# First layer's attention probabilities turned by DMA transposes instead of on the tensor engine

## The reference

```python
# layer 0, per image, C = 128, N = 1024
h = group_norm(x, gn_w, gn_b)                        # 32 groups of 4 channels
q, k, v = split(qkv_w @ h + qkv_b)                   # 128 channels each
attn = softmax(q.T @ k * C ** -0.5, axis=-1)         # 1024 x 1024
x = x + proj_w @ (v @ attn.T) + proj_b
# layer 1, per image, q and k have 16 channels
q, k, v = Wq @ x + bq, Wk @ x + bk, Wv @ x + bv
attn = softmax(q.T @ k, axis=-1)
x = gamma * (v @ attn.T) + x
```

## Time and profile before

| | |
|---|---|
| median of 3 runs | 1952.1 us |
| profiled execution, span | 1946.7 us |
| median less that span | 5.4 us |
| TensorE matmul busy | 1860.1 us (96%) |
| VectorE busy | 1592.0 us (82%) |
| ScalarE busy | 1479.8 us (76%) |
| GpSimd busy | 1071.3 us (55%) |
| DMA engines, mean | 18 GB/s |

### The profile page before, as it was taken

How to read it: one execution, slowest core, us unless ns; L and a number is a source line. 1 busy time by engine, 2 the same in 40 slices (tenths; PEclk the granted TensorE clock), 3 DMA queues, 4 the chain that set the end, 5 groups by cost and what they waited for, 6 DMA issues and landing times.

```text
span 1946.7 us, 36450 instructions
## 1 busy us (share of the span) xinstructions
PE 1860.1 (96%) x11145; PEld 1124.8 (58%) x11145; DVE 1592.0 (82%) x2707; ACT 1479.8 (76%) x2593; POOL 1071.3 (55%) x1000
## 2 busy tenths in 40 slices
PE   5899999999999999999999999999999999999997
PEld 3455565555565555565555555565655555655554
DVE  5688888888888888888888888888888888888875
ACT  4677778777777778777778777777787778777775
POOL 4455565555655556555555655556555555555533
PEclk9999999999999999999999999999999999999999
DMA  1000000000000000000000000000000000000000
GB/s 35 16 1 22 23 18 22 6 21 22 16 22 22 5 22 22 16 22 22 5 22 22 16 22 15 11 22 16 22 22 5 22 22 16 22 23 7 12 12 23
DMA packets 15898, 34.44 MB, mean 18 GB/s; under 512 B 2896, under 2 KB 3568, under 8 KB 15856
## 3 DMA queue, kind: packets, MB, share of 16 engines
q1 hardware_dynamic: 14704, 33.91, 4.9%
q10 hardware_dynamic: 1152, 0.00, 0.0%
HBM read 17.13 MB, written 16.78 MB: 17 GB/s over the span
## 4 chain that ended last, share of the span: by engine, by line
PE 55%; ACT 14%; issue 14%; DVE 12%; POOL 2%; ACTq 1%; DVEq 1%; DMA 0%; POOLq 0%
PE turned L801 14%; PE side L756 9%; PE side L757 8%; PE side L758 8%; ACT prob L408 7%; DVE nmax L542 4%; PE scores L787 4%; ACT pt_head L419 4%; ACT qk L444 3%; PE side L888 3%; PE scores L756 3%; PE scores L758 3%; PE scores L757 3%; DVE pt_tail L561 2%; DVE qk L622 2%
## 5 line engine op out<-in xcount | busy, mean ns | idle before, releaser
L294 POOL TENSOR_SCALAR prob<-prob,rinv 128x1024 f32<-128x1024 f32 x512 | 572.8, 1119 | 814.1 <-DVE rinv L550 803.1
L419 ACT ACTIVATE pt_head<-turned 128x512 f16<-128x512 f32 x1024 | 611.7, 598 | 238.4 <-PE turned L801 228.9
L561 DVE TENSOR_TENSOR pt_tail<-turned,pt_head 128x512 f16<-128x512 f32 x1024 | 700.3, 684 | 106.6 <-ACT pt_head L419 103.5
L801 PE MATMUL turned<-ident,prob 128*128 128x128 f32 x4096 | 625.9, 275 | 33.7 <-DVE pt_tail L561 17.4
L801 PEld LDWEIGHTS turned<-ident,prob 128*128 128x128 f32 x4096 | 489.4, 141 | 282.0 <-DVE pt_tail L561 123.1
L542 DVE TENSOR_REDUCE nmax<-scores 128x1 f32<-128x1024 f32 x512 | 622.1, 1215 | 20.7 <-PE scores L787 10.4
L408 ACT ACTIVATE prob<-scores,nmax 128x1024 f32<-128x1024 f32 x512 | 571.1, 1115 | 8.1 <-DVE nmax L542 6.3
L756 PE MATMUL side<-pt_head,v_head 128*128 128x512 f16 x1024 | 388.9, 380 | 26.2 <-DVE qk L622 17.6
L757 PE MATMUL side<-pt_tail,v_head 128*128 128x512 f16 x1024 | 388.5, 379 | 0.0
L758 PE MATMUL side<-pt_head,v_tail 128*128 128x512 f16 x1024 | 388.5, 379 | 0.0
L756 PE MATMUL scores<-qk_head 128*128 128x512 f16 x512 | 195.9, 383 | 7.1 <-ACT prob L408 4.8
(11 more groups left out here) (87 smaller groups left out, 1714.4 us busy)
## 6 DMA issues: line engine op xcount, KB each, us to landing
x_raw<-in_x_dram SPq DMA_DIRECT2D x32, 512.0 KB, 3.4
out_dram<-y SPq DMA_DIRECT2D x64, 256.0 KB, 2.3
w_qkv<-in_L_conv_qkv_w_dram SPq DMA_DIRECT2D x3, 64.0 KB, 3.7
w_proj<-in_L_conv_proj_w_dram SPq DMA_DIRECT2D x1, 64.0 KB, 3.6
w_v<-in_L_conv_Wv_dram SPq DMA_DIRECT2D x1, 64.0 KB, 3.5
b_qk<-in_L_conv_bq_dram SPq DMA_DIRECT2D x2, 0.1 KB, 3.0
gnw<-in_L_conv_gn_w_dram ACTq DMA_DIRECT2D x1, 0.5 KB, 4.1
gnb<-in_L_conv_gn_b_dram ACTq DMA_DIRECT2D x1, 0.5 KB, 4.4
```

What stands on the lines that cost most here:

```text
L294: nc.gpsimd.tensor_scalar(prob[layer][:, t % 2, :], prob[layer][:, t % 2, :], rinv[layer][:, t:t + 1], P_UP, ALU.mult, ALU.mult).then_inc( ...
L419: nc.scalar.activation(pt_head[layer][:, t // PER_HALF, PER_HALF * h:PER_HALF * (h + 1), at:at + C], turned[layer][:, :].rearrange("p (j n ...
L561: nc.vector.tensor_tensor(pt_tail[layer][part], turned[layer][:, :].rearrange("p (j n) -> p j n", n=C), pt_head[layer][part], ALU.subtract ...
L801: done = nc.tensor.transpose(turned[layer][:, j * C:(j + 1) * C], prob[layer][:, t % 2, m:m + C], ident[:, :])
```

## The change

It concerns layer 0 (lane 0) alone, with its 260 tiles. GpSimd writes the scaled probabilities as fp16 into a new tile `head_row` instead of in place. VectorE makes the fp16 tail in rows, `tail_row` = `prob` x (`rinv` x 4096) - `head_row`, in one instruction over 128 x 1024, from three operands in SBUF; a small instruction (`scale_up`) forms `rinv` x 4096 first. SP issues a DMA transpose of `head_row` and one of `tail_row` (256 KB each), which write all eight turned blocks into `pt_head` and `pt_tail`. The transposes of lane 0 on TensorE and the head and tail copies out of `turned` for lane 0 are gone. The tail in rows stands at the end of the same slot as the tile's maximum. Lane 1 is as before.

```diff
+CROSSBAR = (0,)
+            def swing(layer, it, k):                       # SP
+                im, t = tile_of(layer, it, k)
+                if no_tile(layer, im, t):
+                    return
+                h, at = t // PER_HALF, (t % PER_HALF) * C
+                sp.wait_ge(row_tailed[layer], im.n * TILES + t + 1)
+                sp.sem_inc(waited_sp, 1)
+                if t % PER_HALF == 0 and not (isinstance(im.n, int) and im.n == 0):
+                    sp.wait_ge(attended[layer], im.n * 2 + h - 1)
+                    sp.sem_inc(waited_sp, 1)
+                for rows, into in ((head_row, pt_head), (tail_row, pt_tail)):
+                    sp.dma_start_transpose(into[layer][:, h, :, at:at + C],
+                                           rows[layer][:, t % 2, :]).then_inc(swung[layer][t % 2][h], 16)
...
+                for k in range(8):                         # SP, body
+                    if k == 1 and not skip(second):
...
+                    if k == 4 and not skip(ahead):
+                        load_x(ahead)
+                    for layer in CROSSBAR:
+                        swing(layer, it, k)
+                    if k == 4 and not skip(first):
...
                 pool.wait_ge(inverted[layer], im.n * TILES + t + 1)       # normalise
                 stand_apart()
+                if layer in CROSSBAR:
+                    before = slot_user(im, t)
+                    if before:
+                        pool.wait_ge(swung[layer][t % 2][before[1] // PER_HALF], swings(*before))
+                        stand_apart()
+                    nc.gpsimd.tensor_scalar(head_row[layer][:, t % 2, :], prob[layer][:, t % 2, :],
+                                            rinv[layer][:, t:t + 1], P_UP, ALU.mult,
+                                            ALU.mult).then_inc(row_headed[layer], 1)
+                    return
...
+            def scale_up(layer, it, k):                    # VectorE
...
+                nc.vector.tensor_scalar(rinv_up[layer][:, t:t + 1], rinv[layer][:, t:t + 1], P_UP, 1.0,
+                                        ALU.mult, ALU.mult).then_inc(scaled_up[layer], 1)
+            def tail_row_out(layer, it, k):
...
+                dve.wait_ge(scaled_up[layer], im.n * TILES + t + 1)
+                dve.wait_ge(row_headed[layer], im.n * TILES + t + 1)
+                nc.vector.scalar_tensor_tensor(out=tail_row[layer][:, t % 2, :], in0=prob[layer][:, t % 2, :],
+                                               scalar=rinv_up[layer][:, t:t + 1],
+                                               in1=head_row[layer][:, t % 2, :], op0=ALU.mult,
+                                               op1=ALU.subtract).then_inc(row_tailed[layer], 1)
...
                     invert(1, it, k)
+                    for layer in CROSSBAR:
+                        scale_up(layer, it, k)
                     extra(it, k, 1)
...
                     pt_tail_out(1, it, k, 1)
+                    for layer in CROSSBAR:
+                        tail_row_out(layer, it, k)
...
                 if t == 0:                                                # attend
+                    if layer in CROSSBAR:
+                        for slot in range(2):
+                            pe.wait_ge(swung[layer][slot][h], im.n * 64 + 64)
+                    else:
+                        pe.wait_ge(pt_tailed[layer], im.n * 16 + 8 * (h + 1))
```

More of the change, by code:

```diff
@@ L134, in build @@
         rinv = [sb(f"rinv{l}", [C, TILES]) for l in range(2)]
+        head_row = [sb(f"head_row{l}", [C, 2, N], F16) for l in CROSSBAR]
+        tail_row = [sb(f"tail_row{l}", [C, 2, N], F16) for l in CROSSBAR]
+        rinv_up = [sb(f"rinv_up{l}", [C, TILES]) for l in CROSSBAR]
         pt_head = [sb(f"pt_head{l}", [C, 2, TILES, HALF], F16) for l in range(2)]
@@ L147, in build @@
         waited_dve = sem("waited_dve")
+        waited_sp = sem("waited_sp")
         zeroed = sem("zeroed")
@@ L185, in build @@
         pt_tailed = [sem(f"pt_tailed{l}") for l in range(2)]
+        row_headed = [sem(f"row_headed{l}") for l in CROSSBAR]
+        row_tailed = [sem(f"row_tailed{l}") for l in CROSSBAR]
+        scaled_up = [sem(f"scaled_up{l}") for l in CROSSBAR]
+        swung = [[[sem(f"swung{l}_{s}_{h}") for h in range(2)] for s in range(2)] for l in CROSSBAR]
         attended = [sem(f"attended{l}") for l in range(2)]
@@ L218, in no_tile, with swings, slot_user @@
             return not 0 <= t < PER_HALF if layer == 0 and last(im) else skip(im)
+        def swings(im, t):
+            return im.n * 64 + 32 * (t % PER_HALF // 2 + 1)
+        def slot_user(im, t):
+            if isinstance(im.n, int) and im.n == 0 and t < 2:
+                return None
+            return (im, t - 2) if t >= 2 else (im.before(2 // 2), t + 6)
         @block.sync
@@ L414, in pt_head_out @@
                 im, t = previous_tile(layer, it, k)
-                if no_tile(layer, im, t):
+                if no_tile(layer, im, t) or layer in CROSSBAR:
                     return
@@ L809, in attend @@
                 if t == 0:
-                    pe.wait_ge(pt_tailed[layer], im.n * 16 + 8 * (h + 1))
+                    if layer in CROSSBAR:
+                        for slot in range(2):
+                            pe.wait_ge(swung[layer][slot][h], im.n * 64 + 64)
+                    else:
+                        pe.wait_ge(pt_tailed[layer], im.n * 16 + 8 * (h + 1))
                     if layer == 0:
@@ L972, in _ @@
                 attend(1, end.before(2), 0, t)
-            pe.wait_ge(pt_tailed[0], IMAGES * 16 + 8)
+            for slot in range(2):
+                pe.wait_ge(swung[0][slot][0], IMAGES * 64 + 64)
             pe.wait_ge(qk1_tailed, IMAGES * 2)
```

25 lines of the change are left out of this document (15 added, 10 removed).

## The result

The changed kernel takes 2117.3 us (median of 4 runs, 2116.5 to 2119.0) against 1952.1 us: ratio 1.085, 95% interval 1.083 to 1.086. It is 165 us slower, where 1875 us was predicted, and outside the predicted range.

The account below looks back on a forecast made before the run. TensorE (56.2 of 59.0 us an iteration) was taken as the bound, passing to VectorE's order. 31 iterations x -2.9 = -90 and edges +13 gave a span of 1870, with 5.4 around it 1875 us; range 1785 to 2090.

Parts of the forecast that it names:

- TensorE as the bound: One middle iteration of the kernel before: TensorE's work sums to 56.2 of 59.0 us, 2.8 us lost to waits.
- VectorE's slot and the port: VectorE's slot after the change: 5.81 us by order, 6.52 with `tail_row` waiting for GpSimd's SBUF port.
- the base slot: A slot of the changed kernel without extra work, such as slot 6: 6.52 us, bounds 5.81 and 7.7.
- The rival of GpSimd's other instructions: GpSimd's instructions besides the scalings take the port too: 63 us an iteration, 2090 us, or 59.6 and 1984; chance 0.12.
- The port's sum: Port waits over the eight slots of an iteration: 55.4 us with the port, 53.0 without.
- The iteration: A full iteration of eight slots: 55.4 us plus 0.7 makes 56.1, 2.9 us less than 59.0.
- for coupling between engines I add 0.7: Allowance per iteration for engines waiting on each other: 0.7 us, where it was 2.8 before.
- The edges: First 12 slots, lane 0 alone: `head_row` and `tail_row` stand between exponential and next maximum, +13 us.
- The transposes: SP's DMA transposes, a pair per tile: landing after 3.2 us, hidden under a slot and before `attend`, cost 0.
- The choice of small packets' price: DMA transposes' 256-byte rows: 14 + 12 ns each rather than 104 ns, so 3.2 us a pair instead of 13.3.
- The rival with a chance of 0.17: SP's queue, each tile: transposes bound the slot; 13.3 us a pair gives 3460 us, 9 us gives 2340; chance 0.17.
- hold a pair for little: SP's queue, slots 0 and 4: loads and stores waiting for GpSimd delay a transpose pair only little.

Follow-up runs that it names:

- less_pe: The kernel before with one of four fp32 transposes per half of lane 0's tiles left on TensorE (first tile whole): 1895.7 us (0.971).
- no_tail: The changed kernel, unpadded, without `tail_row` and `scale_up`, both DMA transposes turning `head_row`: 1741.5 us (0.892).
- pad_after: The changed kernel with 32 semaphore increments ahead of VectorE's list, nothing else changed: 2059.3 us (1.054).
- no_port: pad_after with `tail_row` in two halves of 512 whose second operand is a zeroed PSUM bank instead of `head_row`: 2015.6 us (1.031).
- gn_first: pad_after with `tail_row` behind the group norm steps of slots 2, 5 and 7 instead of ahead of them: 2005.9 us (1.027).
- two_gn: pad_after with gn_first's order and lane 1's transposes alternating two PSUM banks, one of them lane 0's unused bank: 1969.4 us (1.009).
- third_turn: pad_after with a third DMA transpose for each tile, of `tail_row` into a spare tensor nobody reads: 2065.3 us (1.057).
- tail_lag: pad_after with `tail_row` and its two DMA transposes one slot later, behind maximum 0 of the next tile: 2301.1 us (1.177).
- pad_before: The kernel before with 40 semaphore increments ahead of VectorE's list, nothing else changed: 1981.2 us (1.015).
- act_head: two_gn with `head_row` made by ScalarE in place of GpSimd, and `scale_up` right behind reciprocal 0: 2031.1 us (1.040).
- tail_mid: pad_after with `tail_row` right behind `scale_up`, ahead of the extra work and lane 1's second half tail: 2069.4 us (1.061).

## Why the prediction was wrong

*TensorE as the bound (the first step, wrong).* The sum of its work, 56.2 of 59.0 us, was right and the conclusion from it was not. An iteration was read as one stage. By slots, TensorE had 6.1 to 7.8 us of work where the slots took 6.1 to 8.7. Slots 0, 3 and 5 had 0.7 to 1.8 us of slack; less_pe shows 1.9 of 5.2 us given back. This count of slack does not say which slot gives back: slot 0 gave 0.62 us and slot 3 nothing. The busy share of 96% could not tell: the matmul rows overlap (0.38 us each at a step of 0.22), so little idle time appears between them. With all three engines relieved and no tail, 6.75 us an iteration is what there was to gain (no_tail against before). What comes then costs 9.8. So 59.0 - 6.75 + 9.8 = 62.1, pad_after's iteration.

*VectorE's slot and the port (number of the base slot right, in part by luck).* Slot 6 was put at 6.52 and measured 6.64, slot 0 at 6.95 and 7.06. `tail_row` alone takes 1.28, step 1.19 to 1.20, at the upper bound; its mean is 1537 ns, as a locked port makes it. But slot 6 is not made up as forecast. `tail_row` was to be due at 4.68 and held by the port until 5.39, with `x1_out` inside that wait. The end of slot 6 in pad_after, where the slot begins at 1043.88:

```profile
1047.91 0.69 DVE L716 SCALAR_TENSOR_TENSOR x<-side,xb 128x512 f32<-128x512 f32 x1
1048.52 0.68 DVE L629 TENSOR_TENSOR pt_tail<-turned,pt_head 128x512 f16<-128x512 f32 x1
1049.12 1.48 DVE L616 SCALAR_TENSOR_TENSOR tail_row<-prob,rinv_up,head_row 128x1024 f16<-128x1024 f32 x1
1050.52 2.34 DVE L590 TENSOR_REDUCE nmax<-scores 128x1 f32<-128x1024 f32 x2
```

`x1_out` costs its full 0.61 ahead of `tail_row`, which starts at 5.24 and loses only 0.2 to the port. Without the port (no_port) the slot is still 6.55, where the forecast had 5.81. In slots 1, 4 and 5 `tail_row` starts after 6.2 us or more and loses nothing to GpSimd (step 1.19). The rival of GpSimd's other instructions holds in part: `xb` goes from 1118 to 2112 ns. The port's sum was about right: 1.4 us of an iteration by no_port and up to 2.4 by the estimate there, where the forecast had held 2.4 (55.4 against 53.0).

*The iteration (wrong, the largest term).* Predicted 55.4 + 0.7, measured 62.1 without the code stall: 6.0 us, 31 x 6.0 = 186 us. With the 58 us of code this is 244 us of the 242 between 1875 and 2117. Slots 1, 2, 4, 5 and 7 are 0.6 to 1.0 over, slot 3 is 2.6 over; together the slots are 6.7 over. The term that failed is "for coupling between engines I add 0.7". It costed the V tails, the short group norm steps and the waits around them at next to nothing. no_tail shows the size: 9.8 us of an iteration hang on `tail_row` and `scale_up`. How it comes about is shown for slot 4: a half tail of lane 0 had filled the wait between the V tails; the same work in one block after it fills nothing. For slots 1, 2, 5 and 7 that is argued, and no run parts it. Of slot 3, 1.95 us is one misplaced instruction, `gn_third` behind `tail_row`. It takes 0.15 us and was costed at nothing, but a PSUM bank hangs on it. gn_first and two_gn get 1.85 and 3.05 us of an iteration back by order and banks alone.

*Code (missing).* 58 us of the 165 by which the kernel is slower are VectorE's loop crossing one more block of code. No term, no rival and no bound held it. It comes from 46 more instructions ahead of the loop's start and 8 more in it; what these instructions do has no part in it.

*The edges (right at the start).* For the first 12 slots +13 was predicted (its six terms add to 5.1, not 5.2, which makes 12), and they measure +11.8; the first 16 have +16.5, and +12.8 in two_gn. The end of the program, some 7 us longer behind the last full iteration, had no term.

*The transposes (right).* Landing 3.2 us forecast, 3.2 measured; throughput hidden (third_turn). The 1309 ns a block that the Trainium skill gives (VectorE: DVE Perf Modes, "The three transpose paths") would have made 20.9 us a tile; a tile with three transposes goes through in a slot of 7.8 us. That the skill has transposes as fast as plain DMAs (Advanced Engine Details and Errata, "X-Bar Transpose (TRN2)") fits only within a factor of two: the plain transfers move 33.9 MB in 4.9% of 1947 us, 2.8 us for a MB, and the 136.4 MB of transposes added take some 35.5% of 2115 us, 5.5 us for a MB. The choice of small packets' price from the earlier trace rows was what carried this step (26 ns a packet taken, a median of 18 and a mean of 22 measured). The rival with a chance of 0.17 fell. That SP's loads "hold a pair for little" holds for the change as made, where the pair that `attend` needs stands ahead of the load of x; in tail_lag, where it stands behind, the load holds it for 7 us.

*What stays open.* two_gn remains 17 us above before (21 between the profiled spans: 13 in the first slots, 2 in 28 iterations, the rest at the start and the end). Whether a further place for `tail_row`, or tail_lag's place with SP's load behind the pair, would take it below was not tried, and no kernel run here that keeps layer 0's heads and tails whole beats the one before.

## What to carry to other kernels

Sum work by slot, not by iteration, and compare each slot with its own length: an engine that is full on average may bind in some of its slots only, and then only a part of the work taken off it comes back. Small half steps that stand in an engine's waits cost little; the same work in one block at the end of the serial round costs most of its length, so ask of each moved instruction which wait it had been filling, and of each short one behind it who waits for it. Ask the same of a DMA queue: what stands ahead of a transfer, and whom that waits for. When an edit changes an engine's number of instructions, look at the instruction queue's packets and at "issue" waits at the loop's branch before believing in any mechanism: semaphore increments as padding tell it apart in one run.

## What the runs showed of the hardware

- VectorE's loop in four blocks of 128 instructions instead of three: 3.7 us of stand-still in each pass (2.8 to 3.1 in pad_before), 79 to 81 instruction packets instead of 19 to 21, and a granted clock of 0.53 to 0.60 for the 8 us after TensorE had idled. ScalarE, with 318 instructions in the loop (act_head), stands still for up to 1.6 us; with 321 in the kernel before it does not.
- A DMA transpose of 128 x 1024 fp16 from SBUF to SBUF: 1024 packets of 256 bytes, a median of 18 ns each, 1.2 to 1.3 us of the queue's issuing, landing after 3.2 us; two a tile fill 40% of the DMA engines, three 59%.
- The port lock runs both ways: GpSimd's 1118 ns becomes 2125 on average when `tail_row` nearly always starts first (tail_mid), and VectorE's 1.28 us becomes 1.79 in the row at 1045.73 above, where GpSimd started first. With a PSUM operand in place of one in SBUF it is gone (1118 ns again). By the Trainium skill (SBUF — State Buffer, "SBUF: two separate sides") whoever starts first has the port for its whole instruction, and the trace agrees.
- A queue holds its transfers in order: in tail_lag a pair of transposes whose input was ready at 1025.4 was issued at 1032.4, behind a load that waited for GpSimd.
